# Attention on one core: the context product from VectorE to GpSimd, mask rows made once, 32 steps written out

## The reference

```python
xt = jnp.transpose(x, (0, 2, 1))                  # 16 x 512 x 256
q = xt @ Wq.T                                     # queries, keys and values alike
qh = q.reshape(B, T, NH, dk).transpose(0, 2, 1, 3)   # 8 heads of 32
scores = scale * jnp.einsum('bhqd,bhkd->bhqk', qh, qh)
logits = (scores * cmask + (1.0 - cmask) * NEG) * rmask
attn = jax.nn.softmax(logits, axis=-1)
ctx = jnp.einsum('bhqk,bhkd->bhqd', attn, qh)
out = ctx.transpose(0, 2, 1, 3).reshape(B, T, D) @ Wo.T
```

## Time and profile before

| | us |
|---|---|
| three runs, median (lowest to highest) | 2059.78 (2058.6 to 2061.94) |
| the profiled execution | 2059.99 |
| its span, first to last instruction | 2058.2 |
| PE busy, share of the span | 1922.2 (93%) |
| DVE busy | 1082.7 (53%) |
| ACT busy | 709.4 (34%) |
| POOL busy | 620.0 (30%) |

### The profile page before, as it was taken

How to read it: one execution, slowest core, us unless ns; L and a number is a source line. 1 busy time by engine, 2 the same in 40 slices (tenths; PEclk the granted TensorE clock), 3 DMA queues, 4 the chain that set the end, 5 groups by cost and what they waited for, 6 DMA issues and landing times. The chain is left out here.

```text
span 2058.2 us, 30150 instructions
## 1 busy us (share of the span) xinstructions
PE 1922.2 (93%) x10324; PEld 1416.7 (69%) x10325; DVE 1082.7 (53%) x1723; ACT 709.4 (34%) x1276; POOL 620.0 (30%) x444
## 2 busy tenths in 40 slices
PE   4999999999999869899999999979999999999995
PEld 2444444444444347799999999868888888888874
DVE  3788878887888548443444433343423323242334
ACT  1566666666666623232333332231010101011000
POOL 3556566666665526211111111100101001010101
PEclk6899999999999969999999999989999999999998
DMA  7776767676765063422333232162302112130204
GB/s 125 111 115 100 111 96 130 101 108 98 128 90 73 21 226 97 150 91 100 124 124 111 83 115 82 67 182 73 102 21 82 41 61 66 36 102 0 93 26 143
DMA packets 117831, 195.83 MB, mean 95 GB/s; under 512 B 11264, under 2 KB 43008, under 8 KB 117776
## 3 DMA queue, kind: packets, MB, share of 16 engines
q1 hardware_dynamic: 106736, 158.94, 34.4%
q0 software_dynamic: 11040, 36.18, 6.1%
HBM read 100.68 MB, written 43.25 MB: 70 GB/s over the span
## 5 line engine op out<-in xcount | busy, mean ns | idle before, releaser
L420 DVE TENSOR_REDUCE maxcol<-ps_m 128x1 f32<-128x512 f32 x512 | 336.9, 681 | 138.5 <-PE ps_m L562 133.4
L337 ACT ACTIVATE e<-ps_e 128x512 f32<-128x512 f32 x512 | 297.3, 596 | 186.5 <-PE ps_e L557 185.7
L148 POOL TENSOR_TENSOR e<-e 128x2048 f32<-128x2048 f32 x64 | 225.6, 3524 | 179.0 <-ACT e L337 178.9
L1384 DVE TENSOR_TENSOR s_h_f<-s_silu,s_ps_u 128x512 f32<-128x512 f32 x77 | 52.9, 688 | 393.5 <-PE s_ps_u L1456 344.0
L562 PE MATMUL ps_m<-kside,qside 97*128 97x512 f32 x512 | 224.3, 443 | 34.7 <-DVE maxcol L420 19.1
L1326 POOL DMA_INDIRECT s_chosen<-routed,s_slot_now x64 | 61.6, 962 | 620.9 <-DVE s_total L1430 609.6
L557 PE MATMUL ps_e<-qside,kside 98*128 98x512 f32 x512 | 236.8, 465 | 3.3 <-ACT e L337 2.1
L557 PEld LDWEIGHTS ps_e<-qside,kside 98*128 98x128 f32 x512 | 96.8, 190 | 191.8 <-ACT e L337 158.7
L1352 ACT ACTIVATE s_silu<-s_ps_g 128x512 f32<-128x512 f32 x77 | 46.0, 598 | 528.8 <-PE s_ps_g L1456 521.3
L1053 DVE TENSOR_TENSOR e_h_f<-e_silu,e_ps_h 128x256 f32<-128x256 f32 (+1 forms) x108 | 45.2, 418 | 250.1 <-ACT e_silu L894 250.1
L562 PEld LDWEIGHTS ps_m<-kside,qside 97*128 97x128 f32 x512 | 101.1, 197 | 80.6 <-DVE maxcol L420 54.6
(11 more groups left out here) (233 smaller groups left out, 4189.0 us busy)
## 6 DMA issues: line engine op xcount, KB each, us to landing
routed<-e_y SPq DMA_DIRECT2D x36, 512.0 KB, 2.8
kside<-q_hi SPq DMA_DIRECT2D x64, 256.0 KB
qside<-qm_hi SPq DMA_DIRECT2D x64, 256.0 KB
x_f<-in_x SPq DMA_DIRECT2D x16, 512.0 KB, 3.5
kside<-q_lo SPq DMA_DIRECT2D x32, 256.0 KB
qside<-qm_lo SPq DMA_DIRECT2D x32, 256.0 KB
attn<-xo SPq DMA_DIRECT2D x32, 256.0 KB, 3.4
keep_rows<-attn SPq DMA_DIRECT2D x8, 1024.0 KB, 5.6
```

The source lines that it names most:

```text
L148: eng.tensor_tensor(into, into, e[k + 1][:, heads, :], ALU.add).then_inc(done, 1)
L337: act.activation(e[kb][:, g, :], ps_e[g % 2][:, :], ACT.Exp, scale=SCALE).then_inc(e_done, 1)
L420: dve.reduce_max(maxcol[par][:, g * KB + kb:g * KB + kb + 1], ps_m[g % 2][:, :], AX.X).then_inc(max_done, 1)
L1384: dve.tensor_tensor(h_f[:], silu[:], ps_u[:], ALU.mult).then_inc(h_done, 1)
```

## The change

1. `c_f` of unit `u - 2` is computed by POOL as its first instruction of step `u`. DVE keeps the four reciprocals. The semaphore `rd_done` becomes `over_done`, and `c_done` now comes from POOL.
2. On ACT, `context_high` moves from behind tile (0, 1) to behind tile (0, 2) of the step. `copy_denominators` waits for `c_done` of two units before.
3. The mask rows of all 16 batches are loaded once (`rows_f`, 16 x 512), and `row_mask` and `row_neg` are made of them with two DVE instructions before the weights are split. SP's stacking transfers take row `b` of them. The per-batch casts on DVE and SP's waits for them go.
4. `run_units` writes out all steps; the loop, the helper `alone` and the register values go.

```diff
+    rows_f = sb("rows_f", [NB, T], f32)
+    row_mask, row_neg = sb("row_mask", [NB, T], f32r), sb("row_neg", [NB, T], f32r)
...
+    def run_units(step, before, after):
+
+        for u in range(before, NU + after):
+            step(u // RING, u % RING)
...
         load_x(0, 0)
+        sp.dma_start(rows_f[:], mask).then_inc(mask_rows_in, 16)
         sp.dma_start(wq_f, wqT.rearrange("(k p) c -> p k c", p=P)).then_inc(w_in, 16)
...
-                alone(sp, q_split, w + 1, w_in, 32)
-                upto(sp, rows_done, 2 * (b + 1))
+                upto(sp, q_split, w + 1)
...
-                                 words(src[bp][0:1, :]).rearrange("p (a t) -> p a t", a=1).to_broadcast([1, HG, T])).then_inc(stack_in[slot], 16)
+                                 words(src[b:b + 1, :]).rearrange("p (a t) -> p a t", a=1).to_broadcast([1, HG, T])).then_inc(stack_in[slot], 16)
...
     @block.gpsimd, step:
+            if known(i, n, -2):
+                w, par = u - 2, n % 2
+                pool.wait_ge(over_done, PARTS * (w + 1))
+                pool.wait_ge(num_done, w + 1)
+                upto(pool, chi_done, w - 1)
+                pool.tensor_tensor(c_f[par][:], num[par][:], den[par][:], ALU.mult).then_inc(c_done, 1)
             if known(i, n, -1):
                 add_pair(pool, u - 1, 1, slice(HG // 2, HG), pair_pool)
...
     @block.scalar, copy_denominators and step:
             act.wait_ge(den_mm, 2 * (w + 1))
+            upto(act, c_done, w - 1)
...
-                    if (kb, g) == (0, 1) and known(i, n, -2):
+                    if (kb, g) == (0, 2) and known(i, n, -2):
                         context_high(i, n)
...
     @block.vector:
+        dve.wait_ge(mask_rows_in, 16)
+        dve.tensor_copy(row_mask[:], rows_f[:]).then_inc(rows_done, 1)
+        dve.tensor_scalar(row_neg[:], rows_f[:], -NEG, NEG, ALU.mult, ALU.add).then_inc(rows_done, 1)
         dve.wait_ge(w_in, 32)
...
-            if n % 2 == 0 and known(i, n, 4):
-                b, bp = 2 * i + (n + 4) // 2, n // 2
-                dve.wait_ge(mask_in[bp], 16 * (i + 2))
-
-                if known(i, n, 1):
-                    dve.wait_ge(stack_in[(n + 1) % RING], 16 * STACK_DMAS * (i + (n + 1) // RING + 1))
-                dve.tensor_copy(row_mask[bp][:], mask_b[bp][0:1, :]).then_inc(rows_done, 1)
-                dve.tensor_scalar(row_neg[bp][:], mask_b[bp][0:1, :], -NEG, NEG, ALU.mult, ALU.add).then_inc(rows_done, 1)
...
-                    if g % 2 == 1 and known(i, n, -1):
-                        normalise(i, n, 2 * kb + g // 2 - KB)
-                        if kb == KB - 1 and g == HG - 1:
-                            normalise(i, n, PARTS)
+                    if g % 2 == 1 and kb >= 2 and known(i, n, -1):
+                        at, par = 2 * (kb - 2) + g // 2, (n - 1) % 2
+                        c = slice(at * T // PARTS, (at + 1) * T // PARTS)
+                        dve.wait_ge(den_done, u)
+                        dve.reciprocal(den[par][:, c], den[par][:, c]).then_inc(over_done, 1)
```

More of the change, by code:

```diff
@@ L49, in attention @@
     mask_b = [sb(f"mask_b{n}", [P, T], f32) for n in range(2)]
-    row_mask = [sb(f"row_mask{n}", [1, T], f32r) for n in range(2)]
-    row_neg = [sb(f"row_neg{n}", [1, T], f32r) for n in range(2)]
+    rows_f = sb("rows_f", [NB, T], f32)
+    row_mask, row_neg = sb("row_mask", [NB, T], f32r), sb("row_neg", [NB, T], f32r)
     q_f = [sb(f"q_f{n}", [P, T], f32) for n in range(2)]
@@ L96, in attention @@
     num_done, den_done, chi_done, o_done = sem("num_done"), sem("den_done"), sem("chi_done"), sem("o_done")
-    max_done, c_done, rd_done, rows_done = sem("max_done"), sem("c_done"), sem("rd_done"), sem("rows_done")
+    max_done, c_done, over_done, rows_done = sem("max_done"), sem("c_done"), sem("over_done"), sem("rows_done")
+    mask_rows_in = sem("mask_rows_in")
     xhi_done, x_split, q_split, c_split = sem("xhi_done"), sem("x_split"), sem("q_split"), sem("c_split")
@@ L107, in upto @@
             eng.wait_ge(s, value)
[L109 to L133, removed]
+    def run_units(step, before, after):
+        for u in range(before, NU + after):
+            step(u // RING, u % RING)
     def known(i, n, off=0, lo=0, hi=NU):
-        if isinstance(i, int):
-            return lo <= RING * i + n + off < hi
-        return True
+        return lo <= RING * i + n + off < hi
     def add_pair(eng, u, pair, heads, done):
@@ L157, in load_x @@
             upto(sp, q_split, UPB * (b - 1))
-            upto(sp, rows_done, 2 * (b - 1))
             upto(sp, x_split, b - 1)
@@ L169, in _ @@
         sp.dma_start(gate_w[:, :, 0:NE], gates.rearrange("(k p) e -> p k e", p=P)).then_inc(gate_in, 16)
+        sp.wait_ge(rows_done, 2)
         sp.wait_ge(setup, 3)
@@ L205, in step @@
                         sp.dma_start(attn[bass.ds(b * D + half * P, P), :], xo[half][:, :]).then_inc(stored[half], 16)
-        run_units(sp, step, -4, 4)
+        run_units(step, -4, 4)
         for half in range(KT):
@@ L254, in _ @@
         pool.tensor_tensor(x_lo[:], x_f[0][:], x_hi[:], ALU.subtract).then_inc(x_split, 1)
-        run_units(pool, step, -4, 2)
+        run_units(step, -4, 2)
     @block.scalar
@@ L371, in _ @@
         act.activation(x_hi[:], x_f[0][:], ACT.Copy).then_inc(xhi_done, 1)
-        run_units(act, step, -4, 5)
+        run_units(step, -4, 5)
     @block.vector
     def _(dve):
[L376 to L391, removed]
         dve.memset(one_f[:], 1.0).then_inc(dve_set, 1)
@@ L431, in step @@
                                     ps_o[:, KT * P:KT * (P + NE)].rearrange("p (h e) -> p h e", h=KT)).then_inc(lg_done, 1)
-        run_units(dve, step, -4, 5)
+        run_units(step, -4, 5)
     @block.tensor
@@ L582, in step @@
                         denominators(u, 0)
-        run_units(pe, step, -4, 5)
+        run_units(step, -4, 5)
 def experts(nc, ctx, sems, keep, attn, w_gate, w_up, w_down, sw_gate, sw_up, held, routed):
```

1 line of the change is left out of this document (removed).

## The result

| | before | after |
|---|---|---|
| median of the runs, us | 2060.39 (2058.6 to 2061.94) | 2041.14 (2037.68 to 2043.55) |
| ratio, 95% interval | | 0.9906 [0.9888, 0.9923] |
| profiled execution, us | 2059.99 | 2043.55 |
| its span, us | 2058.20 | 2041.7 |
| VectorE busy, us | 1082.7 | 1022.2 |

The change is 19 us faster by the medians and 16.4 us by the profiled executions; 2046.4 was forecast, with a range of 2039 to 2056. The changed kernel ran once more beside the experiments (e4) and took 2038.15 there, 21.6 us less than before in the same set and just under the range.

The account below looks back on a forecast made before the run. PE was taken to bound the kernel, waiting at step heads for DVE maxima behind the product and casts. Even steps 7.2, step 2 5.4, loop 2.0, end -0.6, start -0.4 sum to 13.6: 2059.99 to 2046.4 us, range 2039 to 2056.

Parts of the forecast that it names:

- What bounds the kernel: Attention step heads: PE, busy nine tenths or more, waits for DVE maxima queued behind the product and the casts.
- Even steps, 7.2 us: Even steps 4 to 26: third tile to the tile behind the numerators falls from 4.62 to 4.02, 12 x 0.60 us.
- Odd steps, 0: Odd step heads: ACT's chain with the later `c_hi` keeps the tile distance at 4.02 us, gain 0; bounds -0.54 to +0.48.
- The later `c_hi` takes back most of what could be gained: ACT, step heads: `c_hi` between third and fourth exponential takes back most of an odd step's possible 0.48 us.
- Step 2, 5.4 us: Stop near 104 us: 9.85 against 4.02 is 5.83; 0.4 off for late POOL leaves 5.4, bounds 0 and 5.8.
- The loop, 2.0 us: Five loop iterations written out: four steps take 82.31 instead of 82.71, 0.40 us each time; bounds 0 and 2.0.
- The start, -0.4: Before PE's first product: the rows' load, issued ahead of the weights, costs 0.4 us; bounds 0 and -0.9.
- the end, -0.6: Last `c_f`, alone before the output projection: 0.69 us on DVE, some 1.29 on POOL, so 0.6 lost.
- the rival that all is got: Step heads reach step 1's 3.54 us: 27 steps give another 0.48, 13 us more, 2033.4; chance 0.12.
- The slow rival: DVE's pair sum waits for POOL's late `c_lo`, every 0.1 us counting in some 30 steps: 2066 to 2085; chance 0.08.

Follow-up runs that it names:

- e1: The kernel before with only its five loop iterations written out as straight code: 2055.95 us, 0.9984 of before.
- e2: The kernel before with steps written out and mask rows cast once; product still on DVE, `c_hi` in its old place: 2043.26 us, 0.9915 of before.
- e7: The changed kernel with two one-row casts (result unused) again on DVE at each even step's head up to step 26: 2044.07 us, 0.9925 of before.
- e3: The changed kernel with the cast to `c_hi` moved back behind the second exponential: 2032.81 us, 0.9869 of before.
- e6: The kernel before with steps written out, rows cast once and `c_hi` behind the third exponential; product still on DVE: 2042.27 us, 0.9912 of before.
- e5: The changed kernel with one extra unused product on POOL each step, between half pair sum and `c_lo`: 2045.99 us, 0.9928 of before.
- e9: The changed kernel with an extra unused POOL product each step, made to wait for `c_hi`, before `c_lo`: 2047.15 us, 0.9932 of before.
- e10: The changed kernel with POOL's order turned, half pair sum first and product behind it: 2051.39 us, 0.9953 of before.
- e8: The changed kernel with `c_hi` in its old place, rows' load and cast behind the weights', last product on DVE: 2032.01 us, 0.9860 of before.

## Why the prediction was right, and where it was not

- **What bounds the kernel.** Right. PE waited at the heads for maxima behind DVE's product and casts; with these gone the heads are 3.85 us and the row has left the table. (The `ps_m` at 438.67 is the first product behind the third tile, not the second; the distance of 4.62 us is not touched by that.)
- **Even steps, 7.2 us.** A little more was got: 4.62 to 3.85 is 0.77 a head, 0.06 of it from the written-out loop (e1: 4.56). The text put it down to the casts, and e2, which takes them away alone, does get to 3.90 and saves 7.85 us between steps 3 and 27. But the attribution was only half of it: e7 keeps the casts and moves the product, and gets to 3.85. With the late `c_hi` each edit alone gives nearly the whole at an even head. The limits behind them differ: in e2 PE waits for DVE's maxima, in e7 for ACT's fourth exponential.
- **Odd steps, 0.** The step that failed is "the numerators of the next column need `num`, so PE's next tile stays at 4.02 us". The chain on ACT came as worked out: the fourth exponential starts 445.90 - 444.34 = 1.56 us behind the third tile (forecast 1.58). But the numerators start 447.20 - 444.34 = 2.86 behind it, not 3.03. Before, `num` ended at 419.63 and the numerators started only at 419.84, behind a `ps_m` at 419.41:

```profile
419.41 0.49 PE L562 MATMUL ps_m<-kside,qside 97*128 97x512 f32 x1
419.84 1.07 PE L455 MATMUL ps_num<-e,v 128*32 128x512 f32 x8
```

That `ps_m` needs the fourth maximum of DVE's queue, which began at 416.80 and takes 0.64 us for each: the queue had held the numerators, not `num`. Of the 0.17 some 0.08 is the written-out loop (e1: 3.94 at an odd head); the rest is the product, a term that the text had put at 0.
- **The later `c_hi` takes back most of what could be gained.** Right, and e3 and e6 show it: 3.85 against 3.55, 5 us in the medians and 9 in the attention part of the traces, and nothing where the product is on DVE.
- **Step 2, 5.4 us.** 5.80 (23.95 to 18.15), of which 0.29 is lost again by step 3. The 0.4 taken off for a late POOL was seen as 0.32 us at the denominators. The product of 0.79 us, which the text counted with the stop, ran while the clock was at 0.50: part of the 5.8 us is the clock, which no longer falls there.
- **The loop, 2.0 us.** 1.5 in the trace of e1. Its median, 3.8 us lower, says more, with an interval from 1.4 to 5.4; that profiled execution also reached its first full pair sum 2.6 us earlier (71.47 against 74.11), for a reason that stays open. The granted clock was higher there (0.74 from 40 to 60 us, where it had been 0.53), but it doesn't order the executions: from PE's first product to that pair sum e1 took 61.36 us, and the changed kernel, at a clock of 1.00, took 62.08.
- **The start, -0.4; the end, -0.6.** -0.67 and -0.6. The first is within the scatter of the starts (10.28 to 11.36 us with the rows' load ahead; 10.11, 10.47 and 10.69 without), so no run shows the term. And the casts, put at nothing, were not free: one met POOL's `x_lo` and took 2.55 us instead of 0.41. In the changed kernel's two executions the weights were later still, but in e2, e3, e5 to e7, e9 and e10 DVE splits them right behind the casts, without a wait.
- **The sum.** The lead at the full pair sums runs 0.67 us at step 0, 6.49 at step 2, 6.20 at step 3, 17.35 at step 27, 16.65 at step 31; the last `c_hi` comes 15.3 us earlier and the end 16.4. Between steps 3 and 27 it grew by 11.15 where 9.2 was forecast: 1.54 from the loop (e1), 7.85 from the casts (e2) and 1.76 from the product together with the later `c_hi`. That is the miss, in the direction of the rival that all is got. The other differences are no work of the edits: PE was 0.67 us late at its first product and 0.67 ahead at step 0, 1.55 us were lost to the fall of the clock at 682 us, and 1.1 us came from behind the attention. The medians are 5.7 us (8.0 in e4) better than the 13.6 forecast, and the terms above explain only a part of that. That 2041.14 lies inside the range is in part luck, and 2038.15 lies outside it. The order of the forecasts was right: 3.85 lies between 4.02 and 3.54.
- **The slow rival.** Its mechanism is real (step 2, e5, e9), its price was far too high: an overlap of 0.45 us costs PE 0.07 us a step and not 0.1 for every 0.1, since the sum on DVE pays only 0.30 and PE has slack before the denominators.

## What to carry to other kernels

When two engines' delays end at the same wait, price them together with the limit behind them. Here, with `c_hi` late, each edit alone gave 0.7 us at an even head and both together hardly more, since ACT's exponential came next. With `c_hi` early that limit is gone, and both together reach 3.55 us (e3) where the casts' removal alone stays at 3.90 (e2). The product moved with the casts kept and `c_hi` early was not run. Before a small operation is moved on the engine that is next in line, look for its gaps: behind the second exponential `c_hi` was free, one tile later it cost 5 us of a change worth 27. A version with the product on GpSimd and `c_hi` in its old place runs at 0.986 to 0.987 of the kernel before.

## What the runs showed that I had not expected

- A DVE addition, product or cast that starts while a POOL `TENSOR_TENSOR` runs, with its inputs in SBUF, pays what is left of POOL's instruction, less 0.12 to 0.15 us. The half pair sum lost 0.30 in 0.45 us of overlap (e9) and 0.52 in 0.65 (step 2 after); `c_f` in e2 started with 1.28 left (POOL's half sum ends at 424.71) and took 1.82 instead of 0.69, 1.13 more; `row_neg`, a cast of 512 elements in 16 rows that takes 0.41 us alone (e8), started with 2.27 left of POOL's `x_lo` and took 2.55, 2.14 more. In e9 at step 2 the sum started with 0.41 left of the spare product, `c_lo` right behind it went first as well, and the sum paid 1.53. Maxima, which read PSUM, and the reciprocals (0.94 us) paid nothing beside POOL.
- The time behind the attention part is not constant although nothing there was edited: from the last `c_hi` to the end of the span it was 1338.7 us before, 1337.6 after, 1333.7 in e4, 1333.3 in e7 and 1339.7 in e9. Differences of a few us between single profiled executions mean nothing here: the median of a kernel, or the steady steps, must carry a reading. The clock has a part in this in the last steps of the attention too, where it falls to 0.50 for some 3 us in one execution of the changed kernel and not in the other. The steady steps of the attention repeat within 0.1 us (four steps: 80.79 after, 80.86 in e4).
